# The matrix build of a graph network kernel: degrees as columns of a matrix product, evictions of two accumulators, and an address table in lines of sixteen

## The reference

```python
agg = segment_sum(edge_weight[:, None] * x[src], dst)      # first network, two layers
deg = segment_sum(1, dst_with_loops); dinv = deg ** -0.5    # second network
out = segment_sum((x @ W)[src] * dinv[src] * dinv[dst], dst_with_loops)
```

## Time and profile before

| | us |
|---|---|
| median of three runs | 2538.76 (2533.85 to 2540.4) |
| the profiled execution's own time | 2536.82 |
| its span | 2535.1 |
| matrix build, first matmul to end of the last eviction | 823 |
| PE busy over the span | 2090.7 |
| DVE busy | 1101.7 |
| ACT busy | 622.0 |
| POOL busy | 321.2 |

### The profile page before, as it was taken

How to read it: one execution, slowest core, us unless ns; L and a number is a source line. 1 busy time by engine, 2 the same in 40 slices (tenths; PEclk the granted TensorE clock), 3 DMA queues, 4 the chain that set the end, 5 groups by cost and what they waited for, 6 DMA issues and landing times.

```text
span 2535.1 us, 33892 instructions
## 1 busy us (share of the span) xinstructions
PE 2090.7 (82%) x11132; PEld 1612.8 (64%) x11136; DVE 1101.7 (43%) x1823; ACT 622.0 (25%) x1637; POOL 321.2 (13%) x256
## 2 busy tenths in 40 slices
PE   1766666665565677999999999799999998999998
PEld 1455555555555555777777777566677776777776
DVE  6877778888788830111202333322122223222222
ACT  0012344555555631000001111333000001222221
POOL 1002224333444430000000000000000000000000
PEclk8899998988888897999999999899899999999999
DMA  2002224234444455444443333000333341000000
GB/s 70 1 0 65 65 65 129 79 115 129 129 129 129 129 188 174 141 142 142 130 143 129 116 116 118 12 0 0 104 118 128 117 149 34 9 3 10 10 10 9
DMA packets 174593, 221.12 MB, mean 87 GB/s; under 512 B 10300, under 2 KB 155354, under 8 KB 174554
## 3 DMA queue, kind: packets, MB, share of 16 engines
q1 hardware_dynamic: 160234, 213.41, 26.6%
q10 hardware_dynamic: 14320, 7.18, 1.1%
HBM read 135.45 MB, written 85.12 MB: 87 GB/s over the span
## 4 chain that ended last, share of the span: by engine, by line
issue 56%; PE 30%; DVE 7%; ACT 5%; POOL 1%; ACTq 0%; DMA 0%; DVEq 0%; SPq 0%; POOLq 0%
PE ps L1324 11%; PE ps L1405 7%; PE ps L1557 7%; DVE act_c L976 3%; PE ps L1325 3%; ACT ps L555 2%; ACT ring L551 1%; ACT act_b L552 1%; ACT work L552 1%; PE ps L1581 1%; PE ps L1300 1%; DVE work L1262 0%; DVE act_c L972 0%; ACTq L545 0%; DMA ring<-in_edge_weight_dram 0%
## 5 line engine op out<-in xcount | busy, mean ns | idle before, releaser
L1324 PE MATMUL ps<-early,act_c 128*128 128x200 bf16 x3600 | 500.5, 269 | 320.8 <-issue 193.2
L1324 PEld LDWEIGHTS ps<-early,act_c 128*128 128x128 bf16 x3600 | 351.5, 104 | 365.3 <-issue 355.4
L1388 PE MATMUL ps<-ring,act_b 128*128 128x320 f32 x2000 | 545.3, 433 | 0.0
L1388 PEld LDWEIGHTS ps<-ring,act_b 128*128 128x128 f32 x2000 | 378.4, 190 | 153.7 <-issue 0.5
L976 DVE TENSOR_TENSOR act_c<-act_c,pair_tab 128x1024 bf16<-128x1024 bf16 x450 | 355.5, 845 | 0.0
L1325 PE MATMUL ps<-early,act_c 128*128 128x200 bf16 x1200 | 321.2, 268 | 0.0
L1388 PE MATMUL ps<-ring,act_a 128*128 128x320 f32 x1000 | 273.4, 435 | 3.8 <-DMA ring<-weight_matrix 2.2
L551 ACT COPY ring<-ps 128x200 f32<-128x200 f32 x400 | 134.5, 336 | 448.8 <-PE ps L1325 442.8
L1388 PEld LDWEIGHTS ps<-ring,act_a 128*128 128x128 f32 x1000 | 191.1, 192 | 83.5 <-issue 3.6
L972 DVE TENSOR_TENSOR act_c<-rows,pair_tab 128x1024 bf16<-128x1024 bf16 x150 | 146.5, 977 | 156.9 <-PE ps L1325 155.3
L555 ACT ACTIVATE ps<-ones 128x400 f32<-128x400 f32 x400 | 214.3, 536 | 0.0
(11 more groups left out here) (199 smaller groups left out, 1643.6 us busy)
## 6 DMA issues: line engine op xcount, KB each, us to landing
ring<-weight_matrix SPq DMA_DIRECT2D x100, 800.0 KB, 4.3
weight_matrix<-ring SPq DMA_DIRECT2D x20, 2000.0 KB, 8.0
ring<-count_matrix SPq DMA_DIRECT2D x50, 800.0 KB, 4.2
count_matrix<-act_b SPq DMA_DIRECT2D x10, 2000.0 KB, 13.6
count_matrix<-work SPq DMA_DIRECT2D x10, 2000.0 KB, 13.6
x_nodes<-in_x_dram ACTq DMA_DIRECT2D x1, 3072.0 KB
out_dram<-x_nodes SPq DMA_DIRECT2D x4, 640.0 KB
early<-in_L_ffn_w_dram SPq DMA_DIRECT2D x8, 256.0 KB, 5.4
```

What stands on the lines that cost most here:

```text
L1324: nc.tensor.matmul(weights, hot_lane[:, slot, part, two, :, k], hot_key[:, slot, two, :, k], start=False, stop=True, skip_group_check=True)
L1388: i = nc.tensor.matmul(ps[:, 2 * sub + h, 0:SUB], features[:, q * QUADS + t, h * P:(h + 1) * P], ring[:, q, t, :], start=q == 0 and t == 0 ...
```

## The change

- **Degrees.** The key tile gets eight more columns: `pair_dst` (the destination's place in the window) is compared with `dst_wide` by a new DVE instruction per batch, and the counts' matmul is 208 columns wide instead of 200. An accumulator has 408 columns. The last eight are each lane's part of the window's degrees. POOL's tree goes; it copies 160 columns per unit to `degree_part`. The diagonal's one is added by ACT's bias of 1.0 when the degrees are copied.
- **Evictions.** A group is two windows in two neighbouring banks; there are four sets of two. ACT copies both accumulators in one instruction of 816 columns and then zeroes them in one, after waiting for its own copy.
- **Tables.** `line_tab` holds 16 bank addresses and four counts to wait for: PE loads 20 numbers once for two batches. ACT loads ten ends once per unit from rows of twelve.
- **Staging.** `ring`, `act_b` and `work` become parts of one buffer `wide`; each half of the staging (weights, counts and degrees) is contiguous, and the ring lies wholly in the first half. SP loads all five slots of the first streamed unit before the last unit's write, and waits for both writes of the unit before it.
- The prologue gathers the keys in two steps instead of one (six gathers, the same matmuls), and makes two more small tables.

```diff
@@ SP
             sp.wait_ge(unit_complete, BUNITS - 1)
-            write(weight_dram, stage_w[:, 0, :, :], last, 0, weights_written)
-            write(count_dram, stage_c[0], last, 0, counts_written)
+            write(last, 0)
             sp.wait_ge(weights_written[0], 16 + 16 * BUNITS // 2)
+            sp.wait_ge(counts_written[0], 16 + 16 * BUNITS // 2)
             sp.wait_ge(weights_written[1], 16 + 16 * last)
-            early_slots = UNITS // 2
-            for q in range(early_slots):
+            for q in range(UNITS):
                 first_unit(q)
             sp.wait_ge(unit_complete, BUNITS)
-            write(weight_dram, stage_w[:, 1, :, :], last, 1, weights_written)
-            sp.wait_ge(weights_written[1], 16 + 16 * BUNITS // 2)
-            for q in range(early_slots, UNITS):
-                first_unit(q)
-            write(count_dram, stage_c[1], last, 1, counts_written)
+            write(last, 1)
@@ ACT
-                for b in range(ACCS):
-                    act.activation(ps[:, b, 0:2 * WCOLS], zero, ACT.Copy, scale=0.0).then_inc(copies_done, 1)
-                act.wait_ge(copies_done, ACCS)
-                act.sem_inc(acc_free, ACCS - 1)
+                for b in range(SETS):
+                    act.activation(ps[:, b * GROUP:(b + 1) * GROUP, 0:PCOLS], zero, ACT.Copy, scale=0.0).then_inc(acc_free, 1)
...
-                            act.wait_ge(pair_done, ends[k % QUAD])
-                            cols = slice(k * WIN, (k + 1) * WIN)
-                            act.copy(stage_w[:, half, :, cols], ps[:, bank, 0:WCOLS].rearrange("p (t c) -> p t c", t=TILES)).then_inc(copies_done, 1)
-                            act.copy(stage_c[half][:, :, cols], ps[:, bank, WCOLS:2 * WCOLS].rearrange("p (t c) -> p t c", t=TILES)).then_inc(copies_done, 1)
-                            act.wait_ge(copies_done, ACCS + 2 * w)
-                            act.activation(ps[:, before_bank, 0:2 * WCOLS], zero, ACT.Copy, scale=0.0).then_inc(acc_free, 1)
+                            act.wait_ge(pair_done, ends[k])
+                            act.copy(stage[half][:, :, k * GCOLS:(k + 1) * GCOLS].rearrange("p r (b j) -> p b r j", b=GROUP),
+                                     group_ps.rearrange("p b (r j) -> p b r j", j=WIN)).then_inc(copies_done, 1)
+                            act.wait_ge(copies_done, u2 * (2 * UGROUPS) + half * UGROUPS + k + 1)
+                            act.activation(group_ps, zero, ACT.Copy, scale=0.0).then_inc(acc_free, 1)
@@ POOL
-                    pool.wait_ge(acc_free, ACCS + UWINS * (s * 4 + step + 1))
+                    pool.wait_ge(acc_free, SETS + UGROUPS * (s * 4 + step + 1))
...
-                    pool.wait_ge(pool_chain, count(4))
+                    pool.tensor_copy(degree_part[:, ds(s * SCOLS + step * UCOLS, UCOLS)], stage[half][:, 2 * TILES, :]).then_inc(pool_chain, 1)
+                    pool.wait_ge(pool_chain, count(5))
                     pool.sem_inc(unit_complete, 1)
-                    c = stage_c[half]
-                    pool.tensor_tensor(deg_tmp[:, :, :], c[:, 0:12, :], c[:, 12:24, :], ALU.add).then_inc(pool_chain, 1)
...
@@ DVE
-                        dve.tensor_tensor(hot_key[:, slot], for_each(key_wide, WCOLS), of_pairs(pair_key[:, first], WCOLS), ALU.is_equal)
+                        dve.tensor_tensor(hot_key[:, slot, :, 0:WCOLS, :], for_each(key_wide, WCOLS), of_pairs(pair_key[:, first], WCOLS), ALU.is_equal)
+                        dve.tensor_tensor(hot_key[:, slot, :, WCOLS:KCOLS, :], for_each(dst_wide, WIN), of_pairs(pair_dst[:, first], WIN), ALU.is_equal)
@@ PE
-                            quad_tab[:, ds((g * (BATCH // QUAD) + quad) * (QUAD + 1), QUAD + 1)], engines=(mybir.EngineType.PE,), min_val=0, max_val=(ACCS - 1) * 512,
+                            line_tab[:, ds(line * LINE_COLS, LINE_COLS)], engines=(mybir.EngineType.PE,), min_val=0, max_val=(ACCS - 1) * 512,
...
-                                nc.tensor.matmul(counts, hot_lane[:, slot, 0, two, :, k], hot_key[:, slot, two, :, k], start=False, stop=True, skip_group_check=True).then_inc(pair_done, 1)
+                                weights, counts = ps_flat[:, ds(bank, WCOLS)], ps_flat[:, WCOLS:8 * 512][:, ds(bank, KCOLS)]
```

More of the change, by code:

```diff
@@ L64 @@
 QUAD = 4
+LINE = 16
+LINE_QUADS = LINE // QUAD
+LINE_COLS = LINE + LINE_QUADS
+ENDS = 12
 ACCS = 8
+SETS = ACCS // GROUP
 EXPERTS = 4
@@ L235, in build_program @@
         assert at + 2 * WINDOWS + 1 <= KD * PADDED
[L236 to L239, removed]
+        stage = [wide[:, half * ROWS * UCOLS:(half + 1) * ROWS * UCOLS].rearrange("p (r c) -> p r c", r=ROWS) for half in range(2)]
         degree_part = dinv_row
@@ L556, in _ @@
-                act.drain().then_inc(acc_free, 1)
+                        _, ends = nc.values_load_multi_w_load_instructions(
+                            end_tab[:, ds(u2 * (2 * ENDS) + half * ENDS, UGROUPS)], engines=(mybir.EngineType.Activation,), min_val=1, max_val=PPAD + SLOTS * BATCH,
+                            skip_runtime_bounds_check_because="the table counts the pairs up to a group's end, and SLOTS * BATCH more")
+                        for k in range(UGROUPS):
+                            first_bank = (half * UGROUPS + k) % SETS * GROUP
+                            group_ps = ps[:, first_bank:first_bank + GROUP, 0:PCOLS]
+                            act.wait_ge(pair_done, ends[k])
[3 more added lines that the diff above has]
+                            act.activation(group_ps, zero, ACT.Copy, scale=0.0).then_inc(acc_free, 1)
@@ L596, in _ @@
             act.wait_ge(degree_cols, 1)
-            act.copy(degree, ps[:, 7, 0:TILES]).then_inc(degree_copied, 1)
+            act.activation(degree, ps[:, 7, 0:TILES], ACT.Copy, bias=1.0).then_inc(degree_copied, 1)
             act.wait_ge(dinv_ready, 1)
@@ L1308, in _ @@
                 with pe.Fori(0, BATCHES // UNROLL) as step:
[L1309 to L1319 removed]
+                    for m in range(UNROLL * BATCH // LINE):
+                        line = step * (UNROLL * BATCH // LINE) + m
+                        _, (*banks, f0, f1, f2, f3) = nc.values_load_multi_w_load_instructions(
+                            line_tab[:, ds(line * LINE_COLS, LINE_COLS)], engines=(mybir.EngineType.PE,), min_val=0, max_val=(ACCS - 1) * 512,
+                            skip_runtime_bounds_check_because="the table holds (window mod ACCS) * 512, and a group of windows' number plus one")
+                        for quad, free in enumerate((f0, f1, f2, f3)):
+                            batch, half = (m * LINE + quad * QUAD) // BATCH, quad % (BATCH // QUAD)
+                            pe.wait_ge(acc_free, nc.s_assert_within(free, 1, WINDOWS // GROUP, skip_runtime_bounds_check_because="a group's number plus one"))
+                            if half == 0:
+                                pe.wait_ge(batch_ready, step * UNROLL + batch + 1)
@@ L1320, in _ @@
                             for n in range(QUAD):
-                                two, k = quad * QUAD // 2 + n // 2, n % 2
-                                weights, counts = ps_flat[:, ds(banks[n], WCOLS)], ps_flat[:, WCOLS:8 * 512][:, ds(banks[n], WCOLS)]
+                                slot, two, k = batch % SLOTS, half * QUAD // 2 + n // 2, n % 2
+                                bank = banks[quad * QUAD + n]
+                                weights, counts = ps_flat[:, ds(bank, WCOLS)], ps_flat[:, WCOLS:8 * 512][:, ds(bank, KCOLS)]
```

176 lines of the change are left out of this document (91 added, 85 removed).

## The result

| | before | after |
|---|---|---|
| median of the runs beside each other, us | 2537.9 (4 runs) | 2377.26 (4 runs; 2370.09 to 2380.27) |
| ratio to before, 95% interval | | 0.937 (0.935 to 0.939) |
| span of the profiled execution | 2535.1 | 2367.8 |
| matrix build | 823 | 661 |

The change makes the kernel 6.3% faster. The forecast was 2256, with a range up to 2330: the sign is right and the size is not. 113 us of the miss lie in the build (forecast 548, measured 661). Behind it the profiled execution is 5.3 us shorter than before (forecast 7), so under 2 us of the miss are there.

The account below looks back on a forecast made before the run. It took PE's array plus table loads, and 105 us lost beside POOL's additions, to bound the build. Build 823 to 548 (-275) and -7 behind it took 2536.8 to 2255, stated as 2256 us; range 2220 to 2330.

Parts of the forecast that it names:

- What bounds the kernel now: In the build: PE's array plus table loads, 4.5 to 4.8 us a batch, and some 105 us lost beside POOL.
- The quiet regime: Build stretches between units with POOL idle: PE's array plus table loads bind, not DVE, 4.5 to 4.8 us a batch.
- Some 105 us: Build time lost after units, 5.4 to 6.6 us 19 times, while POOL's additions slow DVE's products.
- PE: In the build: one load of 20 numbers per two batches takes 1.45 us, giving 3.32 us a batch.
- DVE, ACT: In the build: DVE 3.44 us a batch; ACT 1.83 us a group, 18.8 to 19.1 us a unit.
- POOL, the step that failed: In the build: the tree's 105 us go; the remaining additions and copy cost 0.5 us a unit, 10 in all.
- Writes and coupling: In the build: the write chain costs 3 us (0 to 10), loops waiting for each other 15 us (3%).
- After the build: Layer loads behind the build: ring slot five at +10 instead of +19 us; saves 7 us, bounds -15 and +5.
- A: Rival on PE's table load: each register has its price, 4.9 us a load; 2475 us; 12% with values towards the forecast.
- C: Rival on PE's table load: 0.305 us a number, 6.1 us a load; slower, total 2563 us; 3%.
- B: Rival in the build: evictions bind, a group costs 2.2 to 2.3 us or a half comes free late; 2290 us; 16%.
- other: Any outcome outside the forecast and its three named rivals; 2%.

## Why the prediction was wrong

By its own steps:

- **What bounds the kernel now.** The quiet regime (array 2.94 us and a gap of loads) was right, the other was not. "Some 105 us" put to POOL's additions beside DVE did not go when the tree went (0.998); what is slow in both kernels there is the table loads beside a write. The check "150 x 4.8 + 105 = 825" confirmed nothing: with the 4.6 us a batch of the earlier trace rows the two stretches lose 6.7 and 6.0 us, 19 times that is some 120, and the sum is 810. It would also have come out with any other owner of the 105.
- **PE.** Right: 1.361 for 1.45. What it lacked: the same load beside a write takes up to 4.6 us, and 10 of 75 take over 2 (24 of 75 in the version without POOL's additions that is full).
- **DVE, ACT.** Right: 3.4 us a batch from 110 to 190, 0.839 and 0.853 us. Groups of two windows and four sets cost nothing that shows: with POOL idle PE's waits on the zeroing in the loop are under 10 us.
- **POOL, the step that failed.** It read "at worst each blocks DVE for its length, 2 us x 20 = 40; at best nothing; 10". It priced a delay of DVE only. DVE was hardly delayed (55 of the 150 comparisons of 64 elements were drawn out, 10 us in all); POOL was, by 57 us, 43, and then 8 to 14 in most units, and the write, ACT, PE and DVE behind it. Measured: 93 us (661 against 568). The rows of before could not show it, as DVE paused in each batch there. But the step took as given that the small additions would still get in once those pauses were gone, and the forecast itself was that they would go. The bound should have been: at worst POOL waits until DVE stops, and DVE stops when ACT has no half.
- **Writes and coupling.** 538 without POOL's 10, measured 568 with POOL idle: 30 too few. Its last seven units take 21.7 us on average where ACT's 19.1 was taken, and ACT waits there for PE; slow loads beside writes are of that size (36 us go with half of the writes), but the 30 are not taken apart further. In the changed kernel these units take 25.3 on average, in turns 17 and 33 to 38 and the last 22. The chain "just fits" only where POOL's 3 us in it hold; they were 57.
- **After the build.** -7 forecast, -5.3 measured in the profiled execution, but by luck and not by the way forecast. Up to the first sums it is +1.7. The rest of the program is 7.0 shorter (1526.4 us from the first sums on against 1533.4, at a granted clock of 0.98 against 0.97), which no term had. SP's loads of the ring stand behind the writes of the unit before, which was late by the same shut-out. With POOL idle the layer loads start 4 us behind the build (676.3 against 672.3), so the reordering works where it isn't blocked.
- **The sum.** 2255 + 83 (POOL) + 30 (writes and coupling) + 2 (after the build) = 2370, the profiled execution's own time. It is the fastest of four; their median lies 7 us above.
- **The rivals.** A and C are out by the load's 1.361. B foresaw the place (a half comes free late) at 16%, though not the cause: its groups at 2.2 us don't exist, and its 582 for the build is 79 below the 661. Only the 2% of "other" were left for an engine that is starved. The prediction's own sign of being wrong, a build over 600 us, came true.

## What to carry to other kernels

When a change takes the pauses out of DVE, look for every GpSimd instruction with two SBUF inputs that something waits for: before the change it costs 0.3 to 0.9 us here, after it mostly up to 3.8 (about a batch of DVE), and in two units 42 and 57, until DVE stopped. Price such an instruction by who waits behind it, not by what it takes from DVE, and move it to another engine or write it without reading. And before a loss is put to one of two things that happen at the same time, find a row in which only one of them happens.

## What the runs showed of the hardware

- A two-input GpSimd addition of 128x128 issued beside gapless DVE instructions with two inputs waited 56.7 us, one of 128x64 in the third unit 41.7; the memsets of a unit's four blocks took 0.47 us together, a copy of 160 columns mostly 0.3 to 5 and once 35.2. Where such a wait ended without a stop of DVE (in the changed kernel and in the two runs that keep the copy), it ended at DVE's comparison of 64 elements, which took 0.27 to 0.48 us instead of 0.19. Whether DVE's two inputs, or the shortness of that comparison, are needed for it was not tried.
- The times of register loads fit a price of some 0.3 us per aligned run of four numbers: 0.305 us for one run (ACT), 0.585 for five numbers from an aligned start, 0.994 for ten (ACT) and 1.361 for five runs. Five numbers from an unaligned start take 1.232: before, the 66 loads under 0.9 us are all at every fourth row. In lines of 20 it is 0.068 us a number; the Trainium skill ("Runtime: NRT & Kernel Launch", section "Instruction fetch mechanics") has some 0.2 us a register, for loads from device memory.
- Some of the same loads take 3 to 4.7 us while a unit's 4 MB are being written, on PE and once on ACT (3.719 for 0.994).
- Copying or zeroing two neighbouring PSUM banks in one instruction costs ScalarE 0.839 and 0.853 us for 816 columns, in line with the rates of the earlier trace rows.
